# Experts' tiles of 256 rows, with the first weights copied by ScalarE

## The reference, cut to what matters

```
probs = softmax(mla_out @ router_w + router_b)
topw, topi = top_k(probs, 2);  topw = topw / (topw.sum(-1) + 1e-8)
combine = sum(one_hot(topi, 8) * topw[..., None], axis=-2)
h1 = gelu(einsum('bsd,edf->ebsf', mla_out, w1) + b1)      # 8 experts, 256 -> 512
h2 = einsum('ebsf,efd->ebsd', h1, w2) + b2                # 512 -> 256
moe_out = einsum('bse,ebsd->bsd', combine, h2)
return hs + 0.3 * moe_out
```

## Time and profile before

| | us |
|---|---|
| median of 3 runs | 4307.8 (4300.36 to 4310.11) |
| profiled execution | 4303.44, span 4301.7 |
| busy in the span | PE 3569.5, DVE 3346.4, ACT 2312.5, POOL 1348.1 |
| `compute`: first x load, first transposes | 3800.1, 3803.0 |
| first and last collect | 3821.1, 4151.1 |
| last scatter issued | 4153.9 |

### The profile page before, as it was taken

One profiled execution on the slowest core, in us unless ns is written; L12 is line 12 of the kernel. 1 busy time (PEld: TensorE's weight loads), 2 busy tenths in 40 slices (PEclk: granted clock), 3 DMA queues, 4 the chain that ended last, 5 costly groups with the idle time before them and its releaser, 6 DMA issues. The chain is left out here.

```text
span 4301.7 us, 64980 instructions
## 1 busy us (share of the span) xinstructions
PE 3569.5 (83%) x19727; PEld 2087.7 (49%) x19728; DVE 3346.4 (78%) x4247; ACT 2312.5 (54%) x4132; POOL 1348.1 (31%) x873
## 2 busy tenths in 40 slices
PE   8968888889449968877779999999999996569950
PEld 3445555555335557767723333333333333459950
DVE  8959999999764456665588989988898874758868
ACT  6855555554764432220028888888888883123323
POOL 4449888889003332220000000000000002744430
PEclk9989999999779979988869999999999996579985
DMA  6754444443767842228512222223232203422249
GB/s 212 254 202 167 162 166 163 161 167 123 266 204 179 195 119 68 68 68 226 162 41 54 68 58 64 67 55 71 51 72 52 70 8 101 135 70 91 90 150 294
DMA packets 534073, 536.92 MB, mean 125 GB/s; under 512 B 84720, under 2 KB 439792, under 8 KB 533664
## 3 DMA queue, kind: packets, MB, share of 16 engines
q1 hardware_dynamic: 507328, 475.20, 37.5%
q0 software_dynamic: 13952, 37.74, 2.6%
q10 hardware_dynamic: 12544, 20.98, 1.9%
HBM read 317.41 MB, written 215.19 MB: 124 GB/s over the span
## 5 line engine op out<-in xcount | busy, mean ns | idle before, releaser
L2131 DVE TENSOR_REDUCE at_top<-at_psM 128x1 f32<-128x1024 f32 x1024 | 1205.9, 1219 | 136.5 <-PE at_psM L1982 135.5
L2091 ACT ACTIVATE at_probs<-at_psS 128x512 f32<-128x512 f32 x2048 | 1060.9, 603 | 250.6 <-PE at_psS L2008 250.5
L2008 PE MATMUL at_psS<-at_q,at_k 64*128 64x512 f32 x2048 | 794.8, 468 | 8.3 <-ACT at_probs L2091 8.3
L575 POOL TENSOR_TENSOR sc_prod<-sc_state,sc_c_row 128x1024 f32<-128x1024 f32 x256 | 709.1, 2789 | 117.8 <-DVE sc_state L724 109.6
L1982 PE MATMUL at_psM<-at_k,at_q 62*128 62x512 f32 x2048 | 689.4, 451 | 36.3 <-DMA at_vraw<-scratch_vf 22.1
L724 DVE TENSOR_TENSOR_SCAN sc_state<-sc_dec,sc_psI 128x1024 f32<-128x1024 f32 x256 | 578.4, 2280 | 53.9 <-PE sc_psI L645 30.0
L1982 PEld LDWEIGHTS at_psM<-at_k,at_q 62*128 62x128 f32 x2048 | 312.8, 190 | 601.9 <-DVE at_top L2131 519.4
L2021 PE MATMUL at_psV<-at_probs,at_v 128*32 128x512 f32 x4096 | 546.3, 605 | 0.0
L656 PE MATMUL sc_psY<-sc_prod,sc_ident 128*128 128x512 f32 x1024 | 466.7, 596 | 3.5 <-DVE sc_y L710 2.2
L606 ACT ACTIVATE sc_dec<-sc_dt,sc_a_exp 128x1024 f32<-128x1024 f32 x256 | 293.6, 1148 | 311.3 <-DVE sc_state L724 308.5
L2008 PEld LDWEIGHTS at_psS<-at_q,at_k 64*128 64x128 f32 x2048 | 337.4, 184 | 195.8 <-ACT at_probs L2091 191.3
(11 more groups left out here) (394 smaller groups left out, 5068.9 us busy)
## 6 DMA issues: line engine op xcount, KB each, us to landing
sc_c_row<-scratch_bc SPq DMA_DIRECT2D x128, 512.0 KB, 4.1
scratch_xs<-at_zeros SPq DMA_DIRECT2D x140, 264.0 KB, 4.6
sc_b_row<-scratch_bc SPq DMA_DIRECT2D x64, 512.0 KB, 5.1
ec_y<-scratch_ys SPq DMA_DIRECT2D x32, 512.0 KB, 6.8
ex_x<-scratch_xs SPq DMA_DIRECT2D x39, 264.0 KB, 3.3
si_x<-in_x SPq DMA_DIRECT2D x16, 512.0 KB, 4.4
scratch_xn<-si_xn SPq DMA_DIRECT2D x16, 512.0 KB, 5.1
scratch_x_t<-si_xT SPq DMA_DIRECT2D x16, 512.0 KB, 5.7
```

The costliest lines, as they stand in the source:

```text
L575: pool.tensor_tensor(prod[:, (n * H + h) % 8, :], state[slot][:], c_row[n % ROWS][:], ALU.mult).then_inc(prod_ready, 1)
L2008: pe.matmul(psS[v % 3][:], rows_of(k4[j], h, 0, GROUP)[:, c * P:(c + 1) * P], rows_of(q4[j], h, 0, GROUP)[:, half * TILE:(half + 1) * TILE ...
L2091: act.activation(probs[:, slot(j, v), :], psS[v % 3][:], ACT.Exp).then_inc(act_done, 1)
L2131: dve.tensor_reduce(top[j % 2][:, h, c:c + 1], psM[t % 2][:], AX.X, ALU.max, negate=True).then_inc(maxed, 1)
```

## The change

Tiles of `compute` have `ETILE` = 256 rows: 64 + 7 = 71 tiles. All buffers and the route's arithmetic follow. The two weight copies per tile go from VectorE's `front` to ScalarE, behind the gelus, and with them ScalarE loads the expert's number once more. `collect` and `store` are no longer in halves: one addition of 128x512 and two scatters per tile. `psY` alternates by the tile's parity. The core of the diff:

```diff
-TILES = 2 * N // TILE + E - 1
+ETILE = 2 * P
+ESUB = ETILE // P
+TILES = 2 * N // ETILE + E - 1
...
-                    for half in two:
-                        pool.wait_ge(y_ready, 2 * i + half + 1)
-                        m.settle(pool)
-                        for s in range(2 * half, 2 * half + 2):
-                            pool.indirect_dma_start(
+                    pool.wait_ge(y_ready, i + 1)
+                    m.settle(pool)
+                    for s in range(ESUB):
+                        pool.indirect_dma_start(
...
+                def first_weights(i, par):
+                    e = expert(i)
+                    for part in two:
+                        src = K.w1[part][:].rearrange("p e f -> p (e f)")[:, bass.ds(e * FF, FF)]
+                        act.activation(w1[par][part][:], src.bitcast(F32), ACT.Copy).then_inc(w1_ready, 1)
...
                     if ahead >= 1:
                         hidden(i + 1, 1 - par)
+                    if ahead >= 2:
+                        first_weights(i + 2, par)
 
                 turn_head(0, 0)
+                first_weights(0, 0)
                 turn_head(1, 1)
+                first_weights(1, 1)
                 hidden(0, 0)
...
                     pe.wait_ge(hid_rest, 2 * i + 2)
-                    for half in two:
-                        later(pe, y_ready, 2 * (i - 1) + (half + 1))
-                        for n in two:
-                            ss = slice((half * 2 + n) * P, (half * 2 + n + 1) * P)
+                    later(pe, y_ready, i - 1)
+                    for n in range(ESUB):
+                        ss = slice(n * P, (n + 1) * P)
...
                 def front(i, par):
-                    e = expert(i)
                     later(dve, hid_psum, FT * (i - 1))
-                    for part in two:
-                        src = K.w1[part][:].rearrange("p e f -> p (e f)")[:, bass.ds(e * FF, FF)]
-                        dve.tensor_copy(w1[par][part][:], src.bitcast(F32)).then_inc(w1_ready, 1)
...
                 def place(i, par):
-                    later(dve, y_st[par], (i - par) * 32)
+                    later(dve, y_st[par], (i - par) * 8 * ESUB)
...
-                    for half in two:
-                        dve.wait_ge(out_psum, 2 * i + half + 1)
-                        bias = K.b2[:, bass.ds(e, 1), :].to_broadcast([P, 2, D])
-                        dve.tensor_tensor(y[par][:, 2 * half:2 * half + 2, :], psY[half][:], bias, ALU.add).then_inc(y_ready, 1)
+                    dve.wait_ge(out_psum, i + 1)
+                    bias = K.b2[:, bass.ds(e, 1), :].to_broadcast([P, ESUB, D])
+                    dve.tensor_tensor(y[par][:], psY[par][:], bias, ALU.add).then_inc(y_ready, 1)
```

More of the change, by code:

```diff
@@ L2452, in _ @@
                 then(dve.tensor_tensor(taken[:], first[:], taken[:], ALU.subtract))
-                then(dve.tensor_scalar(tiles_of[:], taken[:], float(TILE - 1), None, ALU.add))
+                then(dve.tensor_scalar(tiles_of[:], taken[:], float(ETILE - 1), None, ALU.add))
                 then(dve.tensor_copy(count[:], tiles_of[:]))
-                then(dve.tensor_single_scalar(count[:], count[:], TILE.bit_length() - 1, ALU.logical_shift_right))
+                then(dve.tensor_single_scalar(count[:], count[:], ETILE.bit_length() - 1, ALU.logical_shift_right))
                 then(dve.tensor_copy(tiles_of[:], count[:]))
@@ L2463, in _ @@
                 then(dve.tensor_tensor(start[:], tilenum[:], start[:], ALU.subtract))
-                then(dve.scalar_tensor_tensor(out=start[:], in0=which[:], scalar=float(N // TILE), in1=start[:],
+                then(dve.scalar_tensor_tensor(out=start[:], in0=which[:], scalar=float(N // ETILE), in1=start[:],
                                               op0=ALU.mult, op1=ALU.add))
@@ L2483, in compute @@
         two = range(2)
-        x, y = [m.sb(f"x{k}", [P, SUB, P + 4]) for k in two], [m.sb(f"y{k}", [P, SUB, D]) for k in two]
-        name, slot = [m.sb(f"name{k}", [P, SUB, 2]) for k in two], [m.sb(f"slot{k}", [P, SUB], U32) for k in two]
-        spare, pad = [m.sb(f"spare{k}", [P, SUB]) for k in two], m.sb("pad", [P, 3, SUB])
+        x, y = [m.sb(f"x{k}", [P, ESUB, P + 4]) for k in two], [m.sb(f"y{k}", [P, ESUB, D]) for k in two]
+        name, slot = [m.sb(f"name{k}", [P, ESUB, 2]) for k in two], [m.sb(f"slot{k}", [P, ESUB], U32) for k in two]
+        spare, pad = [m.sb(f"spare{k}", [P, ESUB]) for k in two], m.sb("pad", [P, 3, ESUB])
         ident = m.sb("ident", [P, P])
-        xT = [[m.sb(f"xT{k}{part}", [P, TILE], F32R) for part in two] for k in two]
+        xT = [[m.sb(f"xT{k}{part}", [P, ETILE], F32R) for part in two] for k in two]
         w1 = [[m.sb(f"w1{k}{part}", [P, FF], F32R) for part in two] for k in two]
[L2490 to L2493, removed]
+        whole = [m.sb(f"whole{k}", [P, FT, ETILE]) for k in two]
+        hid = [[m.sb(f"hid{k}{part}", [P, FT, ETILE], F32R) for part in two] for k in two]
+        psT, psH = m.ps("psT", [P, TILE]), [m.ps(f"psH{f}", [P, TILE]) for f in range(FT)]
+        psY = [m.ps(f"psY{k}", [P, ESUB, D]) for k in two]
+        turned_rows = psT[:, 0:ETILE]
         made = m.sem("made")
@@ L2527, in load @@
                     m.settle(sp)
-                    tile = sp.value_load(K.tile_at[0:1, bass.ds(i, 1)], min_val=0, max_val=NT * E + E - 1)
+                    tile = sp.value_load(K.tile_at[0:1, bass.ds(i, 1)], min_val=0, max_val=N // ETILE * E + E - 1)
                     sp.dma_start(x[par][:], at(A["xs"], tile)).then_inc(x_loaded[par], 16)
@@ L2543, in store @@
                     pool.wait_ge(slot_ready, i + 1)
-                    for half in two:
-                        pool.wait_ge(y_ready, 2 * i + half + 1)
-                        m.settle(pool)
-                        for s in range(2 * half, 2 * half + 2):
-                            pool.indirect_dma_start(
-                                out=A["ys"], out_offset=bass.IndirectOffsetOnAxis(ap=slot[par][:, s:s + 1], axis=0),
-                                in_=y[par][:, s, :], in_offset=None).then_inc(y_st[par], 16)
+                    pool.wait_ge(y_ready, i + 1)
+                    m.settle(pool)
+                    for s in range(ESUB):
+                        pool.indirect_dma_start(
+                            out=A["ys"], out_offset=bass.IndirectOffsetOnAxis(ap=slot[par][:, s:s + 1], axis=0),
+                            in_=y[par][:, s, :], in_offset=None).then_inc(y_st[par], 16)
                 identity(nc, pool, ident, made)
                 for k in two:
-                    pool.iota(spare[k][:], pattern=[[P, SUB]], base=1 + 2 * N + k * TILE, channel_multiplier=1,
+                    pool.iota(spare[k][:], pattern=[[P, ESUB]], base=1 + 2 * N + k * ETILE, channel_multiplier=1,
                               allow_small_or_imprecise_dtypes=True).then_inc(made, 1)
@@ L2557, in _ @@
                 for k in two:
[L2558 removed]
+                    pool.wait_ge(y_st[k], 16 * ESUB * ((TILES + 1 - k) // 2))
             @block.scalar
@@ L2567, in turn_head @@
                     later(act, hid_psum, FT * (i - 1))
-                    act.activation(xT[par][0][:], psT[:].rearrange("p s t -> p (s t)"), ACT.Copy).then_inc(x_head, 1)
+                    act.activation(xT[par][0][:], turned_rows, ACT.Copy).then_inc(x_head, 1)
+                def first_weights(i, par):
[3 more added lines that the diff above has]
+                        act.activation(w1[par][part][:], src.bitcast(F32), ACT.Copy).then_inc(w1_ready, 1)
                 def hidden(i, par):
@@ L2572, in hidden @@
                     later(act, hid_rest, 2 * (i - 1))
-                    later(act, out_psum, 2 * (i - 1))
+                    later(act, out_psum, i - 1)
                     for f in range(FT):
                         act.wait_ge(hid_psum, FT * i + (f + 1))
-                        act.activation(whole[par][:, f, :], psH[f][:], ACT.Gelu,
+                        act.activation(whole[par][:, f, :], psH[f][:, 0:ETILE], ACT.Gelu,
                                        bias=K.b1[:, bass.ds(e * FT + f, 1)]).then_inc(hid_ready, 1)
@@ L2596, in turn @@
                     later(pe, x_rest, i)
-                    for s in range(SUB):
-                        last = pe.transpose(psT[:, s, :], x[par][:, s, 0:P], ident[:])
+                    for s in range(ESUB):
+                        last = pe.transpose(psT[:, s * P:(s + 1) * P], x[par][:, s, 0:P], ident[:])
                     last.then_inc(turned, 1)
@@ L2607, in hidden @@
                         xh, xl = (xT[par][part][:] for part in two)
-                        products(pe, psH[f][:], ((wh, xh), (wh, xl), (wl, xh)), True, True).then_inc(hid_psum, 1)
+                        products(pe, psH[f][:, 0:ETILE], ((wh, xh), (wh, xl), (wl, xh)), True, True).then_inc(hid_psum, 1)
                 def output(i, par):
@@ L2613, in output @@
                     pe.wait_ge(hid_rest, 2 * i + 2)
```

(12 more changed lines are left out.)

4 lines of the change are left out of this document (2 added, 2 removed).

## The result

The changed kernel takes 4299.0 us (median of 20 runs, 4292.9 to 4305.6), the kernel before 4306.2 beside it: a ratio of 0.9985, 95% interval 0.9978 to 0.9991. That is 7 us faster, against a forecast that it would be slower. Two more comparisons gave 0.9982 (0.9973 to 0.9991) and 0.9985 (0.9977 to 0.9994). The forecast was 4318; the first rival's figure was 4295.

The account below looks back on a forecast made before the run. TensorE bounded the kernel before; after, the scatter's loop would: 2.76 + 3.1 + 0.2 + 3.98 = 10.04 us for two steps, 5.02 each, so 70 T - 337 adds 14 to 4303.4, giving 4318 (range 4286 to 4341).

Parts of the forecast that it names:

- Rival 1: Experts' stage: scatter lands undisturbed in 2.4 to 2.6 us, VectorE's order bounds; 4.70 a step, -8 us, 4295; chance 0.22.
- the alternating steps: Experts' stage: a late placing delays its x load, so long and short steps take turns, mean 5.02 us.
- the balance: Length of a 256-row step at which the change neither gains nor loses: 4.8 us, from 337/70.
- the loop over the scatter: Collect, two scatters, landing, placing two tiles on, its collect: 10.04 us for two steps, 5.02 a step.
- The landing: Second scatter, issue to landed: 1.2 instruction, 1.44 after it, 0.5 behind the x load; 3.1 us taken.
- Placing to collect: VectorE from a tile's placing (first small operation) to its collect: 3.98 us.
- VectorE's own order: VectorE's instructions of one step: 3.98 placing to collect plus 0.61 to the next placing, 4.59 us; bounds 4.2 to 4.9.
- rival 2: VectorE's chain shorter, scatter's wait small: TensorE's own pace, 4.5 a step, -22 us, 4281; chance 0.13.
- What would show it: Signs: VectorE idle for the scatter's DMA 25 to 35 us in all, alternating collects, TensorE some 90% busy, landing about 3.
- Rival 4: ScalarE's weight copies come after 4.73 us; at +0.3, 4.8 a step, 0 us; chance 0.13 with other ends near 4304.
- The ends: Start and finish of the experts' stage: first collect 6 us earlier, last two steps 2 us shorter.
- the formula 70 T - 337: Stage's time difference in us, T being the new step: 70 T - 2 - 328.8 - 6.2; +14 at T = 5.02.

Follow-up runs that it names:

- the four buffers: Changed kernel with four buffers each of y, slot and spare instead of two, placing waiting for tile i - 4: 4281.2 us, ratio 0.9946 to the kernel before.

## Why the prediction was wrong

The place of the new wait, its releaser, the alternating steps and the side engines were right; the forecast's sign was not, since the balance was 4.81 a step, the forecast 5.02, and what came 4.74. The step that failed is the sum for the loop over the scatter, two steps at 10.04: the loop is the right one (the four buffers show it), but two of its terms were too large. Term by term, from the two steps shown above:

| | forecast | measured |
|---|---|---|
| collect to second scatter's issue | 2.76 | 2.76 |
| its landing and the release | 3.1 + 0.2 | 2.98 |
| placing to collect | 3.98 | 3.73 |
| two steps | 10.04 | 9.47 |

- **The landing, -0.32 in two steps, 11 us in all.** I took 0.5 for standing behind the x load. The scatter does stand behind it in the waiting tile (x data from 3959.0, the scatter's instruction over at 3959.03), but a load of half as many rows is nearly through when the scatter's data comes. Its data starts 0.66 instead of 0.57 after the instruction's end and takes 0.64 instead of 0.51: 0.2 in all, not 0.5. In the other tile the x load goes behind and the landing is 2.4. That alternation was foreseen, its size wasn't. The kernel before with its load moved shows that at full size the mechanism is real.
- **Placing to collect, -0.25 in two steps, 9 us.** The four small operations take 0.74 instead of 0.87: the one on the tile's name takes 0.23, not 0.42. The 0.42 of the earlier trace rows was one tile's; over all tiles of the kernel before that operation takes 0.22 to 0.47 with a median of 0.23, so the step that was read was not a usual one. The gap before xT is 0.22, not 0.3. The collect comes 0.83 after the last subtraction's start, not 0.88. All three were put too high, and the loop adds them.
- **VectorE's own order** was put at 4.59; the step without a wait is 4.27, 0.61 from collect to placing as foreseen and 3.66 from placing to collect instead of 3.98. So the doubt set against rival 2, that three engines have 0.1 to spare, was wrong too: with the wait gone the step is 4.50 to 4.54, TensorE's pace, for which 4.51 was worked out.
- **What would show it.** The wait of 27.9 us lies in the foreseen 25 to 35, but by luck: it is the difference between the loop (5.02 a step) and VectorE's order (4.59), and both were some 0.3 too high. TensorE was foreseen some 90% busy and is 97 to 98.
- **TensorE**: 12 hidden products in 1.42 (3958.22 to 3959.64), 0.118 each, against 0.119 from the row. So halving the columns came close to halving the time, in the rows of this case. The Trainium skill's pair of figures ("TensorE: Matmul & The Clock Gate", "Back-to-back issue gap"), 81 ns at 128 columns and 131 ns at 512, doesn't hold for these float32r products: 0.22 us at 512 columns, 0.118 at 256.
- **ScalarE**: its second weight copy ends 3.5 after the head's start (3953.58 to 3957.05), 3.9 forecast; TensorE's hidden products waited for it once, 0.5 us. Rival 4 did not happen.
- **The ends**: tile 0's second collect before is at 3821.7, 0.6 after its first and not 1.2, so the 38 steps took 329.4 and not 328.8. From first x load to first collect it is 14.6, against 21.7 to that second collect before: 7.1 earlier instead of 6.2. The last steps take off 1.5 instead of 2. Together the formula 70 T - 337 gives -5.3 at 4.739 and the stage has -6.2.
- **Rival 1** gave the nearest figure, 4295 by its T of 4.70, but its mechanism is not what came, so that is luck. It had the scatter landing at 2.4 to 2.6 and VectorE's order as the bound; the late landing was 2.8, VectorE's order needs 4.27, and the scatter's loop is the bound. The range held the time; the chance of faster, 0.24, was too low for a case where the difference is 70 times 0.07 either way.

In the kernel before, 28 of the 39 last scatters met an x load whose data began 0.3 to 0.6 us after their instruction's end, just before their own would have. Their data started when 165 to 354 of the load's 512 pieces had started (median 218), and the load ended 0.7 us or more after that, 1.0 in the median: such a scatter waits for a part of the load, under a half as a rule, and not for all of it. The Trainium skill ("DMA: Bandwidth & Descriptors", "Queues, rings and completion order") says that an engine drains a whole packet of one queue, typically some 9 to 17 descriptors, before it turns to the next. Spread evenly over 16 engines the median of 218 is 14 pieces for each, and 165 to 354 are 10 to 22 (an estimate), so the trace agrees with that in the main. The prediction took the 4.0 of the earlier trace rows as speaking against the rule; it doesn't. In the changed kernel 203 to 256 of the 256 pieces have started when the scatter's data does, but the load began with the end of the scatter's instruction and not 0.5 after it, so the scatter is held for only 0.02 to 0.2 us longer than undisturbed.

## What to carry to other kernels

When tiles are halved, every wait that spans a fixed number of tiles spans half the time: write down for each double buffer the loop from its last writer round to its next, and set its length against two new steps. A loop's length is a sum, so its terms have to be read to 0.05 us where 70 steps turn on 0.07, and from many tiles rather than from one step; and a wait that releases a resource belongs where the resource is written, not at the head of the step. Here two more buffers, or moving the wait down past the divide, was worth twice what the whole change gave.

## What was unexpected of the hardware

A number loaded at run time leaves VectorE idle for 0.87 to 1.05 us where nothing covers it (1.05 in the earlier trace rows, 0.87 and 0.97 with the copies back on VectorE). The load itself is 0.30 of this in most tiles and 0.47 to 0.56 in some. In the changed kernel the collect's load never started before the subtraction that stands ahead of it, but up to 0.09 us after that one's start; with the names' copy set between them it was 0.22 in every second tile, and took 0.48 there, which took back a gain of 0.25.

VectorE's small operation on the tile's name took from 0.22 to 0.47 in the kernel before, and a scatter beside it is not enough for the long time: it depends on where in the scatter it falls. In 14 of 39 tiles it started 0.47 to 0.67 after the start of a scatter's instruction on GpSimd, and then ended only 0.94 after that start, near the end of the instruction's 0.97. In the other tiles it took 0.22 to 0.23, in 23 of them beside a scatter too. In the changed kernel it starts at most 0.3 after a scatter's start, as in the step above (3960.99, beside the scatter of 3960.86), and takes 0.21 to 0.23. Why it is held in that part alone is not shown.
